# Weight tiles laid out and loaded in pairs in a two-layer graph network

## What is computed

```
h = relu(layernorm(x))
feat = concat([h[src], h[dst]], axis=1)            # 8192 x 2048
e_hh = relu(feat[:256]     @ W_hh + b_hh)          # W_*: 2048 x 1024
e_oo = relu(feat[256:1536] @ W_oo + b_oo)
e_ho = relu(feat[1536:]    @ W_ho + b_ho)
logit = concat([e_hh, e_oo, e_ho]) @ W_a + b_a
alpha = softmax of logit over the edges of one dst
z = segment_sum(alpha * h[src], dst)
nf2 = concat([h, z], axis=1)                       # 512 x 2048
x = x + concat([relu(nf2[:128] @ W_hn + b_hn), relu(nf2[128:] @ W_on + b_on)])
h = relu(layernorm(x))
x = x + normalised_adjacency @ (h @ W.T + b)
```

## Time and profile before

| what | value |
|---|---|
| runs | 661.83, 661.90, 663.68 us; median 661.9 |
| profiled execution | 663.97 us, its span 662.2 us |
| mean granted TensorE clock | 0.935 |
| TensorE matmuls | 564.0 us busy, 85% of the span |
| VectorE, ScalarE, GpSimd | 441.9, 288.6, 216.8 us |
| DMA traffic | 140.52 MB in 55974 packets |
| queue of GpSimd (gathers, biases) | 20624 packets, 74.98 MB, 41.7% of the 16 engines' time |
| queue of SP (weights, x, outputs) | 27072 packets, 50.34 MB, 22.4% |
| queue of ScalarE (tables) | 8242 packets, 14.75 MB, 6.0% |

### The profile page before, as it was taken

How to read it: one execution, slowest core, us unless ns; L and a number is a source line. 1 busy time by engine, 2 the same in 40 slices (tenths; PEclk the granted TensorE clock), 3 DMA queues, 4 the chain that set the end, 5 groups by cost and what they waited for, 6 DMA issues and landing times.

```text
span 662.2 us, 8385 instructions
## 1 busy us (share of the span) xinstructions
PE 564.0 (85%) x2376; PEld 417.1 (63%) x2377; DVE 441.9 (67%) x903; ACT 288.6 (44%) x466; POOL 216.8 (33%) x228
## 2 busy tenths in 40 slices
PE   0899999999949895989888898677959999869987
PEld 0788777777626673756566576433637878757866
DVE  6715256675767987877877976676797169883252
ACT  2623311214166464637373555589863174222200
POOL 2000240176675666757654576310020000000000
PEclk9899999999969998898989799788988899969999
DMA  8335383499999999999999999993437055322021
GB/s 315 121 113 187 121 304 133 144 206 335 291 293 319 298 305 311 304 305 316 292 317 299 300 321 304 252 261 119 142 121 292 16 192 182 104 63 64 0 81 48
DMA packets 55974, 140.52 MB, mean 212 GB/s; under 512 B 6274, under 2 KB 6402, under 8 KB 55938
## 3 DMA queue, kind: packets, MB, share of 16 engines
q0 software_dynamic: 20624, 74.98, 41.7%
q1 hardware_dynamic: 27072, 50.34, 22.4%
q10 hardware_dynamic: 8242, 14.75, 6.0%
HBM read 123.27 MB, written 16.78 MB: 212 GB/s over the span
## 4 chain that ended last, share of the span: by engine, by line
PE 41%; DMA 23%; POOL 12%; issue 10%; DVE 8%; ACT 4%; POOLq 1%; DVEq 0%; ACTq 0%
PE ps L609 23%; DMA gath<-tab_a,tabl_s 19%; POOL gath L288 7%; PE ps L595 6%; POOL gath L281 3%; PE ps L768 3%; DMA gath<-tab_b,tabl_s 3%; PE ps L559 3%; PE ps L740 2%; POOL tabl_s L278 2%; PE ps L753 2%; ACT onehot L468 2%; DVE logit_d L889 1%; DVE logit_d L978 1%; PE ps L588 1%
## 5 line engine op out<-in xcount | busy, mean ns | idle before, releaser
L609 PE MATMUL ps<-ring_h,actT_h 128*128 128x512 f32 x520 | 228.8, 440 | 34.3 <-ACT stage L439 14.0
L609 PE MATMUL ps<-ring_h,actT_l 128*128 128x512 f32 x520 | 209.1, 402 | 0.0
L609 PE MATMUL ps<-ring_l,actT_h 128*128 128x512 f32 x520 | 208.7, 401 | 0.0
L468 ACT ACTIVATE onehot<-onehot,lgs 128x512 bf16<-128x512 bf16 x192 | 124.6, 711 | 103.6 <-DVE onehot L871 103.2
L421 ACT CAST ring_h<-raw 128x512 fp32r<-128x512 f32 x176 | 104.8, 615 | 118.0 <-PE ps L609 87.6
L609 PEld LDWEIGHTS ps<-ring_h,actT_h 128*128 128x128 f32 x520 | 101.7, 195 | 69.3 <-ACT stage L439 16.4
L839 DVE TENSOR_TENSOR ring_l<-raw,ring_h 128x512 fp32r<-128x512 f32 x176 | 117.0, 685 | 35.5 <-ACT ring_h L421 35.3
L288 POOL DMA_INDIRECT gath<-tab_b,tabl_s x64 | 105.6, 1650 | 96.4 <-DMA gath<-tab_a,tabl_s 40.7
L854 DVE SCALAR_TENSOR_TENSOR gath<-gath,wa_b 128x1024 f32<-128x1024 f32 x64 | 78.0, 1219 | 67.7 <-DMA gath<-tab_b,tabl_s 67.7
L609 PEld LDWEIGHTS ps<-ring_h,actT_l 128*128 128x128 f32 x520 | 101.1, 194 | 22.8
L609 PEld LDWEIGHTS ps<-ring_l,actT_h 128*128 128x128 f32 x520 | 101.9, 196 | 20.9
(11 more groups left out here) (156 smaller groups left out, 466.9 us busy)
## 6 DMA issues: line engine op xcount, KB each, us to landing
raw<-in_L_gnn_W_ho_dram SPq DMA_DIRECT2D x32, 256.0 KB
raw<-in_L_gnn_W_oo_dram SPq DMA_DIRECT2D x32, 256.0 KB
raw<-in_L_gnn_W_hh_dram SPq DMA_DIRECT2D x32, 256.0 KB
raw<-in_L_gnn_W_on_dram SPq DMA_DIRECT2D x32, 256.0 KB
raw<-in_L_gnn_W_hn_dram SPq DMA_DIRECT2D x32, 256.0 KB
tab_a<-stage ACTq DMA_DIRECT2D x24, 256.0 KB
tab_b<-stage ACTq DMA_DIRECT2D x24, 256.0 KB
raw<-in_L_gnn_W_dram SPq DMA_DIRECT2D x16, 256.0 KB
```

Source lines behind the costliest of these rows:

```text
L468: ins = nc.scalar.mul(onehot[:, s, 1 + i, :], onehot[:, s, 1, :], lgs[:, i, q:q + 1])
L609: mm = nc.tensor.matmul(ps[:, first + m, :], w, v, start=(k == 0 and i == 0), stop=(k == KT - 1 and i == 2))
```

## The change

Outside the program each weight matrix is rearranged, without changing its shape: within a block of 1024 rows the order becomes column half n, pair of row tiles, row p within the tile, member of the pair j, 512 columns. A row of the new array holds row p of two neighbouring row tiles, 4 KB in one piece, and the 128 rows of a pair are 512 KB in one piece. SP loads such a pair with one transfer, ScalarE rounds it and VectorE splits it with one instruction each, and the semaphores count by two. The waits move with it: a load waits until both old tiles are split, a cast until TensorE has freed both slots, a split until the pair is rounded. In the order of each engine the work of a pair stands where the even tile's stood; where the odd tile's stood there is nothing. `raw`, `ring_h` and `ring_l` keep their sizes (4 pairs). TensorE's program is unchanged.

```diff
@@ -63,7 +63,7 @@
-        raw = sb("raw", [P, RAW, FB], F32)
+        raw = sb("raw", [P, RAW // 2, 2, FB], F32)
@@ -141,7 +141,7 @@
-        s_raw = [sem(f"raw_loaded{i}") for i in range(RAW)]
+        s_raw = [sem(f"raw_loaded{i}") for i in range(RAW // 2)]
@@ -220,17 +220,17 @@
             def load(w, row, n, q, k):
 
-                sp.wait_ge(s_low, q * KT + k + 1)
-                sp.dma_start(raw[:, k % RAW, :], w[bass.ds(row + k * P, P), n * FB:(n + 1) * FB]).then_inc(s_raw[k % RAW], 16)
+                sp.wait_ge(s_low, q * KT + k + 2)
+                sp.dma_start(raw[:, k // 2, :, :], w[bass.ds(row + (n * KT + k) // 2 * P, P), :]).then_inc(s_raw[k // 2], 16)
 
             for t, (w, _) in enumerate(KINDS):
                 with sp.Fori(0, 2) as half:
                     for n in range(NN):
-                        for k in range(KT):
+                        for k in range(0, KT, 2):
                             load(w, half * D, n, (half * NN + n) + t * 2 * NN, k)
             q = CH_EDGE
             for w, row, n in [c[:3] for c in NODE[0] + NODE[1]] + [(W1t, 0, n) for n in range(NN)]:
-                for k in range(KT):
+                for k in range(0, KT, 2):
                     load(w, row, n, q, k)
                 q += 1
@@ -416,9 +416,9 @@
             def round_w(q, k):
-                act.wait_ge(s_raw[k % RAW], (q * (KT // RAW) + k // RAW) * 16 + 16)
-                act.wait_ge(s_slot, q * KT + k + 1)
-                nc.scalar.copy(ring_h[:, k, :], raw[:, k % RAW, :]).then_inc(s_high, 1)
+                act.wait_ge(s_raw[k // 2], q * 16 + 16)
+                act.wait_ge(s_slot, q * KT + k + 2)
+                nc.scalar.copy(ring_h[:, k:k + 2, :], raw[:, k // 2, :, :]).then_inc(s_high, 2)
@@ -471,7 +471,8 @@
             def rounds(p, end):
 
                 for i in range(p, end):
-                    round_w(i // KT, i % KT)
+                    if i % 2 == 0:
+                        round_w(i // KT, i % KT)
@@ -518,7 +519,7 @@
                 if k < 4:
-                    round_w(q, k)
+                    rounds(q * KT + k, q * KT + k + 1)
@@ -835,8 +836,11 @@
             def low_w(q, k):
-                dve.wait_ge(s_high, q * KT + k + 1)
-                nc.vector.tensor_tensor(ring_l[:, k, :], raw[:, k % RAW, :], f32(ring_h[:, k, :]), ALU.subtract).then_inc(s_low, 1)
+
+                if k % 2 == 0:
+                    dve.wait_ge(s_high, q * KT + k + 2)
+                    nc.vector.tensor_tensor(ring_l[:, k:k + 2, :], raw[:, k // 2, :, :], f32(ring_h[:, k:k + 2, :]),
+                                            ALU.subtract).then_inc(s_low, 2)
@@ -1102,7 +1106,10 @@
-        a = _np.ascontiguousarray(inputs[name].T if name == "L1_gnn_W" else inputs[name])
+        a = inputs[name].T if name == "L1_gnn_W" else inputs[name]
+        if "_W" in name and a.shape[1] > 1:
+            a = a.reshape(-1, 4, 2, 128, 2, 512).transpose(0, 4, 1, 3, 2, 5).reshape(a.shape)
+        a = _np.ascontiguousarray(a)
```

## The result

The changed kernel is slower: a median of 665.92 us over 20 runs against 663.38 us over 20 runs of the kernel before in the same comparison, a ratio of 1.0037 with a 95% interval of 1.0024 to 1.0051, so about 2.5 us. The forecast was 2.4 us the other way, and the measured 665.92 lies just above the range's upper end of 665.0. Read against the median of 661.9 us of the first three runs the loss would look larger than it is; the wider set of the kernel before goes from 661.42 to 666.24 us.

A forecast was written before the change was run, and what follows sets the result against it. The prediction took the DMA engines to bound the gather stage, with GpSimd's loop close behind. Its terms, 0.7 + 0.8 + 1.0 - 4.9 = -2.4 us, took the median from 661.9 to 659.5 us; range 655.5 to 665.0.

The forecast's parts named there:

- the end: Behind chunk 20: last pair's cast and split delay the first output, for which TensorE waits; +1.0 us, between 0.9 and 1.1.
- the node stage: Chunks of node row tiles: a pair late by one split could cost up to 0.6 us; put at 0.
- The loads' gain: Gather stage: 65.2 loads of 256 KB fall from 0.739 to 0.660 us; -4.9 us, bounds nothing and 10.7.
- The estimate from the Trainium skill: Gather stage weight loads: packet overhead by that page gives a gain of only 1.1 us, making the sum +1.4 us.
- that is hidden, and so is the other side of it: Gather stage: VectorE's idle time hides the 0.05 us saved per pair split and the 1.17 us in every odd step.
- The start: Before the first matmul: tile 0's cast and split become a pair's; +0.7 us, between 0.6 and 0.8.
- The +0.8 us behind the first kind: After the first kind of logits: pair split and casts delay the copy freeing chunk 14's bank; +0.8 us, bounds 0 and 1.1.
- bursts of loads: Gather stage: 512 KB loads lengthen GpSimd's 18 waits, 6 us; +3.6, 665.5 us; with no gain at all 664.4; chance 0.19.
- rival 1: Weight loads: price goes by bytes or packets stay 2 KB; gain 0.5 to 2.9 us, middle 662.9 us; chance 0.22.

The follow-up runs named there:

- cast_pairs: Changed kernel with splits of single tiles, each at its own step of VectorE, casts still in pairs; ratio 1.0006 to the kernel before.
- pairs_only: Changed kernel with the old weight layout, two 256 KB loads of 2 KB rows per pair, casts and splits still in pairs; ratio 1.0039 to the kernel before.
- load_only: Changed kernel with its layout and 512 KB loads kept, but casts and splits of single tiles; 660.52 us against 663.54 for the kernel before, ratio 0.9947.
- edge_single: Changed kernel with single casts and splits in chunks 0 to 15, pairs from chunk 16 on, pair loads throughout; ratio 1.0005 to the kernel before.
- before_early: Kernel before, with the last tile's split of the last chunk put behind the first output in VectorE's order; ratio 0.9984.
- lag4: Kernel before, with the destination gather four tiles behind the source gather instead of three; ratio 0.9993.

## Why the prediction was wrong

The forecast was -2.4 us and +2.5 was measured, 4.9 us apart. By the ratios some 3 of these are in the late part of the program: the sum had +1.0 us for the end and 0 for the node stage, and pairs there cost 3.8 to 4.6 us. The loads' gain was 1.4 us too large. For the edge part the sum had 0.7 + 0.8 us, and pairs there cost 1.4 to 2.1, so little is missing in the total, though it is made up otherwise than I had it.

**The bound was right, and so was the direction of the loads' gain.** The DMA engines set the pace of the gather stage (14.7 us less with half the weights of two kinds), the load of 256 KB fell from 0.739 to 0.670 us (0.660 forecast), and the loads by themselves bring 3.5 us (4.9 forecast, bounds 0 and 10.7). That term was too large by 1.4 us, and 0.6 of these are the price (65.2 loads at 0.069 us less, over 1.05, are 4.3 us). The estimate from the Trainium skill, "DMA: Bandwidth & Descriptors", section "Why small descriptors are slow (HBM only)", was 1.1 us; the 3.5 us measured, with an interval of 2.2 to 4.8, don't agree with it as the whole of the effect.

**The gather stage: "that is hidden, and so is the other side of it".** VectorE has idle time in that stage, and the work moved within it is small, but with the splits in pairs only 0.6 of the 3.2 us at tile 58 are left (368.07 as the mean of four kernels with pair loads and pair splits, 368.0 with old loads, 368.7 before). At chunk 14 more is left: the same four are at 401.2 on average (400.5 to 402.0), four with pair loads and single splits at 400.3 (399.6 to 401.1), three with old loads and single splits at 403.2. So the splits in pairs take about 1 of the 2.9 us that reach chunk 14; with the spread of single executions that size is rough. GpSimd hardly waits for VectorE by the table of waits (destination gathers, 140 to 416 us: 1.3 us before, 2.7 after), which is what I relied on. The cast_pairs run, 365.22 and 399.59, puts it on the splits. By which chain of waits in that stage is open.

**What failed most: the end.** The +1.0 us came as computed (pause 2.92 to 3.97). The sum stopped at the restart of TensorE. What the longer pause does to the clock behind it was not in it: 1.64 us in the profiled execution, and on the average of executions perhaps half of that (an estimate from the 3 of 6 above), since the kernel before loses it part of the time.

**And the node stage, "I put it at 0".** I saw that TensorE takes 0.69 us a tile there and a split 0.61, and gave up to 0.6 us. It cost 1.25 us (28.79 for 27.54). The load of a pair is asked for when both old tiles are split, the cast waits until both are there, and the split until both are cast. The chain of pairs_only shows the stall without pair loads, beginning with the wait for the weights:

```profile
538.99 4.36 DMA raw<-in_L_gnn_W_on_dram
543.50 1.06 ACT ring_h L423
544.65 1.24 DVE ring_l L844
545.93 16.63 PE ps L612 x72
```

Pair loads by themselves do not cause it (27.36 in load_only), and pairs in the late part alone do (28.35 in edge_single); with pair casts and single splits more than half of it is left (28.11 in cast_pairs). How it divides between the late request and the longer cast was not measured further.

**Smaller points.** The start: the split begins where the lows of the activations end, at 24.54, and the first matmul is at 25.86, 1.32 us later for 0.78 before: +0.54, forecast 0.7. In the profile it is hidden, since the transposes ahead of it took 5.10 us instead of 6.48 in that execution. The +0.8 us behind the first kind came out at +0.24: from the last row maximum of the first kind (435.64 us before, 433.13 after) to the first matmul of chunk 14 it is 18.20 us for 17.96. Five kernels with pairs there give 18.20 or 18.21, six with single casts and splits and a distance of three tiles 17.94 to 17.96, and cast_pairs 17.68.

**The rivals.** The one on the slow side was bursts of loads. It was wrong in its mechanism: the DMA share of the stage stayed at 1.04, and long loads alone are the gain. (Its 0.33 us is half of a 256 KB piece, not of the 512 KB load that it speaks of, and its price stands once as 665.5 and once as 664.4 us. The middle of rival 1 is 662.7 us by its own terms, not 662.9.) That the kernel would be slower was in places that the prediction names: 2.5 us of costs which I had, the node stage, which I had looked at and closed at nothing, and the restart of TensorE at the end, where I stopped short of the clock. That the measured time came out only 0.9 us above the range is no merit of the mechanism: no rival had this one.

## What to carry to other kernels

Larger transfers and larger instructions are two changes, and only the first paid here: 4 KB packets with the old instruction size are worth 3.5 us, and the merged instructions cost 6 us on top, where each pair was to save 0.05 to 0.07 us of its engine. When two units of work are merged, list every place where the first unit was the last thing waited for, and every request that goes out when one of them is done; each of those moves by a whole unit, at the start, at every handover and at the end. A pause of TensorE that grows can have a second price, the clock behind it (1.6 us here), so put what restarts it ahead of what it doesn't need yet.

## What the runs showed of the hardware

- The clock after a pause is a matter of chance that depends on its length: at about 1.7 us it stayed at its upper level in 3 of 3 profiled executions, at 2.9 us in 3 of 6, at 4.0 us in 0 of 7. A fall cost 1.6 us.
- Packets of 4 KB gained more under full traffic than alone, in the two stretches compared. Under the gathers a piece of 256 KB went from 0.739 to 0.670 us, 9%; alone, from 590 to 600 us, 62.6% of 10 us for the same 2.10 MB in the kernel after, 0.783 us for 0.825, 5%:

```profile
q1 hardware_dynamic: 576, 2.10, 62.6%
```

- GpSimd's destination gathers, with nothing changed in them, take different times (means of 140 to 416 us): 1.65 us before and 1.69 in before_early, which is the same program up to there; with pair loads and single splits 1.61 to 1.64 in four kernels, with pair loads and pair splits 1.67 to 1.71 in four, and 1.73 us with splits in two halves. The kernel's time doesn't follow them: lag4 has 1.76 us and is as fast as the kernel before.
